# A bidirectional ConvLSTM scan in 128-row products, with shifted taps loaded ahead and the cell in column halves

## What is computed

```python
def step(carry, xr):                       # xr: one row, (16, 48, 32)
    h, c = carry
    inp = jnp.concatenate([xr, h], axis=1)
    gates = lax.conv_general_dilated(inp, w_mid, (1,), 'SAME', dimension_numbers=dn) + b[None, :, None]
    i, f, g, o = jnp.split(gates, 4, axis=1)
    c2 = jax.nn.sigmoid(f) * c + jax.nn.sigmoid(i) * jnp.tanh(g)
    h2 = jax.nn.sigmoid(o) * jnp.tanh(c2)
    return ((h2, c2), h2)
```

## Time and profile before

| | us |
|---|---|
| median of 3 runs (636.04 to 639.83) | 638.73 |
| profiled execution | 642.67 |
| its span, first to last instruction | 640.9 |
| TensorE busy in the span (90%) | 574.0 |
| VectorE (78%), ScalarE (68%), POOL (39%) | 500.4, 435.9, 251.7 |
| chain that ended last, share: TensorE, VectorE, issue, DMA | 47%, 28%, 10%, 6% |

### The profile page before, as it was taken

The page is one execution under the profiler, slowest core; times in us unless marked ns, Lnnn a source line. Parts: engine busy times, 40 slices in busy tenths (PEclk is TensorE's granted clock), DMA queues, the critical chain, the costliest instruction groups (busy, mean ns, idle before and its releaser), DMA issues.

```text
span 640.9 us, 12616 instructions
## 1 busy us (share of the span) xinstructions
PE 574.0 (90%) x3404; PEld 340.9 (53%) x3404; DVE 500.4 (78%) x962; ACT 435.9 (68%) x645; POOL 251.7 (39%) x299
## 2 busy tenths in 40 slices
PE   6993699999999999979979989999999999999970
PEld 1232366666665556555545656666666556555530
DVE  2687669999999979997998657666667677776765
ACT  3771369999999969877886655555555556565645
POOL 2660004333333323333866634444444434343410
PEclk9996689999999979998997999999999999999985
DMA  8857646655656776777531233333322222222316
GB/s 216 260 148 220 185 118 141 140 141 141 141 142 156 153 146 155 145 137 152 132 76 32 48 82 86 80 79 79 78 64 68 76 77 80 78 67 65 96 55 197
DMA packets 101751, 75.77 MB, mean 118 GB/s; under 512 B 52883, under 2 KB 85141, under 8 KB 101381
## 3 DMA queue, kind: packets, MB, share of 16 engines
q1 hardware_dynamic: 100948, 71.69, 45.3%
q10 hardware_dynamic: 768, 3.67, 2.3%
HBM read 48.84 MB, written 22.15 MB: 111 GB/s over the span
## 4 chain that ended last, share of the span: by engine, by line
PE 47%; DVE 28%; issue 10%; DMA 6%; SPq 3%; ACT 2%; DVEq 1%; POOL 1%; ACTq 0%; POOLq 0%
DVE hmax L1242 11%; PE pz L724 10%; PE pz L703 9%; PE pz L718 5%; DVE onehot L1227 5%; PE p_edge L724 5%; PE p_edge L703 4%; DVE idx L1218 3%; PE p_edge L718 3%; PE pz L554 3%; PE pz L632 2%; DMA idx_d<-idx 2%; DMA y_hl<-y_d 2%; DVE val L1210 2%; PE p_keys L546 1%
## 5 line engine op out<-in xcount | busy, mean ns | idle before, releaser
L1242 DVE TENSOR_REDUCE hmax<-gel 96x128 f32<-96x1024 f32 x128 | 151.7, 1203 | 16.6 <-ACT gel L849 16.6
L849 ACT ACTIVATE gel<-pz 96x1024 f32<-96x1024 f32 x128 | 130.5, 1020 | 37.8 <-PE pz L632 27.6
L1119 POOL CAST ht<-h 48x512 fp32r<-48x512 f32 x62 | 37.5, 605 | 141.9 <-DVE h L1353 141.3
L1121 POOL TENSOR_TENSOR ht<-h,ht 48x512 fp32r<-48x512 f32 x62 | 73.5, 1185 | 5.0
L724 PE MATMUL pz<-ht,w_xh 128*112 128x512 f32 x258 | 71.9, 414 | 1.6 <-DMA ht<-xh 1.6
L703 PE MATMUL pz<-xh,w_xh 128*112 128x512 f32 (+1 forms) x258 | 69.1, 404 | 0.0
L632 PE MATMUL pz<-onehot,ab_hi 64*96 64x512 f32 x256 | 61.3, 475 | 4.0 <-ACT gel L849 3.4
L914 ACT ACTIVATE pz<-c 48x512 f32<-48x512 f32 x43 | 25.7, 597 | 48.0 <-DVE c L1346 48.0
L724 PEld LDWEIGHTS pz<-ht,w_xh 128*112 128x112 f32 x258 | 41.9, 175 | 28.4 <-issue 14.7
L703 PEld LDWEIGHTS pz<-xh,w_xh 128*112 128x112 f32 x258 | 45.7, 178 | 16.8 <-issue 0.7
L632 PE MATMUL pz<-onehot,ab_lo 64*96 64x512 f32 x256 | 53.4, 412 | 0.0
(11 more groups left out here) (148 smaller groups left out, 1219.3 us busy)
## 6 DMA issues: line engine op xcount, KB each, us to landing
ib<-idx_d SPq DMA_DIRECT2D x64, 256.0 KB, 4.3
y_d<-y SPq DMA_DIRECT2D x32, 192.0 KB, 3.3
y_hl<-y_d SPq DMA_DIRECT2D x32, 192.0 KB, 4.1
hist_d<-h SPq DMA_DIRECT2D x62, 96.0 KB, 1.9
hp<-hist_d SPq DMA_DIRECT2D x30, 192.0 KB, 2.7
kr<-xn_d SPq DMA_DIRECT2D x32, 98.0 KB
xn_d<-x_in SPq DMA_DIRECT2D x32, 96.0 KB, 2.3
kl<-xn_d SPq DMA_DIRECT2D x32, 96.0 KB
```

The source lines that it names most:

```text
L849: act.activation(gel[:, t % 2], pz[0:O, 2 * (t % 2):2 * (t % 2) + 2, :], ACT.Gelu) \
L1119: pool.tensor_copy(h_slots(ht, 0, d), columns(h2[0:C, d])).then_inc(S["h_top"], 1)
L1121: pool.tensor_tensor(h_slots(ht, HALF, d), columns(h2[0:C, d]), h_slots(ht, 0, d).bitcast(F32), ALU.subtract).then_inc(S["h_lo"], 1)
L1242: dve.tensor_reduce(dst, gel[:, t % 2].rearrange("p w (r c k) -> p w r c k", r=WS, k=KN), AX_X, ALU.max).then_inc(S["maxed"], 1)
```

## The change

The products with 48 rows, `w_e` and `he` are gone. `x_part` becomes two products of 98 rows (three shifted copies of 32 rows of the low part of x and two rows of ones for the bias, in the new tile `xt`). `h_part` has six products on `xh` and six on `ht`, all with 128 rows; the head of h now goes into the low rows of `xh` of the next row, its rest and its rounded copy into `ht`. Before that the low parts of x are stored to DRAM (`store_lows`, `xl_d`); `load_shifts` loads the three shifted copies two steps ahead, `load_thirds` two pieces for `ht` one step ahead. The stores of the lows and the twins of three quarters of the rows move into SP's turns for groups 14 to 21 and 26 to 29, the last quarter into steps 2 to 5. In the turns, y is loaded for g + 4 before the spread. Cell, its tanh (now into `cu`), h and its head are computed in two column halves. All loops of the scan are unrolled. The bias, scaling and splitting of the weights follow the new rows.

```diff
@@ SP @@
+            def store_lows(r, sem):
+                for first, rows, src in ((0, C, 0), (C, HALF - C, HALF + 32)):
+                    sp.dma_start(xl_d[r:r + 2, first:first + rows].rearrange("r c n -> c r n"),
+                                 xh[src:src + rows, r:r + 2, 0:SLOT - 1].bitcast(F32)).then_inc(S[sem], 16)
...
+            def load_shifts(s, d):
+                lows = xl_d[row_of(s, d), 0:32, 0:SLOT - TAPS]
+                sp.dma_start(xt[0:96, d, s % 2, 0:SLOT - TAPS].bitcast(F32),
+                             bass.AP(lows.tensor, lows.offset, [[1, TAPS], [SLOT - 1, 32], [1, SLOT - TAPS]])) \
+                    .then_inc(S[f"x_shifts{d}{s % 2}"], 16)
+            def load_thirds(s, d):
+                for q in range(2):
+                    sp.dma_start(ht[HALF * q + C:HALF * q + HALF, d, 0:SLOT - 1].bitcast(F32),
+                                 xl_d[row_of(s, d), 32 + 16 * q:C + 16 * q]).then_inc(S[f"x_third{d}"], 16)
...
-                for k, stage in ((3, load_y), (0, load_xres), (3, store_idx), (-2, store_x1), (5, load_keys),
+                for k, stage in ((0, load_xres), (3, store_idx), (-2, store_x1), (5, load_keys), (4, load_y),
                                  (3, spread_idx)):
...
+                    if at < 8:
+                        block, part = divmod(at, 4)
+                        sp.wait_ge(S["x1_split"], PAIRS * (block + 1))
+                        store_lows((0, 24)[block] + 2 * part, "xl_stored0")
+                        load_twins((0, 24)[block] + 2 * part, "x_twins0")
+                    if 12 <= at < 16:
+                        sp.wait_ge(S["x1_split"], PAIRS * 3)
+                        store_lows(16 + 2 * (at - 12), "xl_stored1")
+                        load_twins(16 + 2 * (at - 12), "x_twins1")
...
-            def step(s, b):
+            def step(s):
                 for d in range(2):
-                    if not isinstance(s, int) or s + 1 < H:
-                        load_third(s + 1, d)
-                    if isinstance(s, int) and s + 2 < H // 2:
-                        load_twins(s + 2, d, b)
+                    if s + 1 < H:
+                        sp.wait_ge(S["gates"], s * 4 + (2 * d + 2))
+                        load_thirds(s + 1, d)
+                    if s + 2 < H:
+                        load_shifts(s + 2, d)
                     store_h(s, d)
-                    if isinstance(s, int) and 2 <= s < H // 2 + 2:
-                        load_x1r(s - 2, d)
-                if later(s, H // 2 + 1):
-                    load_h(s - 1, 1 - b)
+                    if 6 <= s < H // 2 + 6:
+                        load_x1r(s - 6, d)
+                    if 2 <= s < 6:
+                        (store_lows, load_twins)[d](4 + 2 * s, ("xl_stored1", "x_twins1")[d])
+                if s >= H // 2 + 1:
+                    load_h(s - 1, 1 - s % 2)
@@ TensorE @@
+            def x_part(s, d, k):
+                pe.wait_ge(S[f"x_shifts{d}{s % 2}"], s // 2 * 16 + 16)
+                for m in range(2):
+                    pe.matmul(gate_banks(k, d)[m][0:TOP, :], w_x[0:98, d, m], by_column(xt[0:98, d, s % 2, 0:(W + 1) * B]),
+                              start=True, stop=False)
+            def h_part(s, d, k):
+                if later(s):
+                    pe.wait_ge(S["h_top"], s * 4 + (2 * d - 2))
                 for m in range(2):
                     for t in range(TAPS):
+                        row = xh[:, reg(row_of(s, d), 0, 1), t:t + (W + 1) * B].rearrange("p o n -> p (o n)")
+                        pe.matmul(gate_banks(k, d)[m][0:TOP, :], w_rows[:, 0, d, m, t], by_column(row),
+                                  start=False, stop=False)
+                pe.wait_ge(S[f"x_third{d}"], s * 32 + 32)
                 if later(s):
                     pe.wait_ge(S["h_edge"], s * 2 + (d - 1))
                     pe.wait_ge(S["h_lo"], s * 2 + (d - 1))
                 for m in range(2):
                     for t in range(TAPS):
+                        mm = pe.matmul(gate_banks(k, d)[m][0:TOP, :], w_rows[:, 1, d, m, t],
+                                       by_column(ht[:, d, t:t + (W + 1) * B]), start=False, stop=(t == TAPS - 1))
                     mm.then_inc(S["gates"], 1)
@@ ScalarE @@
             def tanh_cell(s, d, k):
-                act.wait_ge(S["cells"], s * 2 + (d + 1))
-                act.activation(gate_banks(k, d)[1][HALF:TOP, :], c2[HALF:TOP, d], ACT.Tanh, scale=0.5) \
-                    .then_inc(S["tanh_c"], 1)
+                for n, (to, c) in enumerate(zip(column_halves(cu[HALF:TOP, d]), column_halves(c2[HALF:TOP, d]))):
+                    act.wait_ge(S["cells"], s * 4 + (2 * d + 1 + n))
+                    act.activation(to, c, ACT.Tanh, scale=0.5).then_inc(S["tanh_c"], 1)
@@ POOL, h_parts @@
+                for n, h in enumerate(column_halves(h2[0:C, d])):
+                    pool.wait_ge(S["h2_ready"], s * 4 + (2 * d + 1 + n))
+                    pool.tensor_copy(head[:, BX * n:BX * n + BX], columns(h)).then_inc(S["h_top"], 1)
+                pool.wait_ge(S["h_top"], s * 4 + (2 * d + 2))
+                pool.tensor_tensor(h_slots(ht, 0, d), columns(h2[0:C, d]), head.bitcast(F32),
                                    ALU.subtract).then_inc(S["h_lo"], 1)
@@ VectorE, cell @@
+                for to, kept, new in zip(column_halves(c2[HALF:TOP, d]), column_halves(cu[HALF:TOP, d]),
+                                         column_halves(b_if[HALF:TOP, :])):
+                    dve.scalar_tensor_tensor(to, kept, 0.5, new, ALU.mult, ALU.add).then_inc(S["cells"], 1)
...
+                for n, (to, out_gate, cell_tanh) in enumerate(zip(column_halves(h2[0:C, d]),
+                                                                  column_halves(tgo[HALF:TOP, d]),
+                                                                  column_halves(cu[HALF:TOP, d]))):
+                    dve.wait_ge(S["tanh_c"], s * 4 + (2 * d + 1 + n))
+                    dve.scalar_tensor_tensor(to, out_gate, 1.0, cell_tanh, ALU.add, ALU.mult) \
+                        .then_inc(S["h2_ready"], 1)
```

More of the change, by code:

```diff
@@ L428, in turn @@
                     sp.wait_ge(S["x1_hi"], 2 * PAIRS)
[L429 to L432, removed]
-                for k, stage in ((3, load_y), (0, load_xres), (3, store_idx), (-2, store_x1), (5, load_keys),
+                    sp.wait_ge(S["pads_set"], 8)
+                    sp.wait_ge(S["xl_stored0"], 32 * 8)
+                    load_shifts(0, d)
+                    load_thirds(0, d)
+                    load_shifts(1, d)
+                for k, stage in ((0, load_xres), (3, store_idx), (-2, store_x1), (5, load_keys), (4, load_y),
                                  (3, spread_idx)):
@@ L519, in _ @@
-            for s in range(14, 18):
-                step(s, s % 2)
-            with sp.Fori(0, H // 4 - 2) as j:
-                for b in range(2):
-                    step(j * 2 + (18 + b), b)
+            consts = ((wp_sb[:], wp), (wp_low[:], wp[C:O]), (gb_sb[:], gb), (comb_sb[:], comb))
+            for s in range(6, 30):
+                step(s)
+                if s < 10:
+                    dst, src = consts[s - 6]
+                    sp.dma_start(dst, src).then_inc(S["consts2"], 16)
@@ L526, in _ @@
                     .then_inc(S["first_loaded"], 16)
-            step(30, 0)
+            step(30)
             load_h(30, 0)
@@ L707, in h_part @@
                 if later(s):
-                    pe.wait_ge(S["h_top"], s * 2 + (d - 1))
                     pe.wait_ge(S["h_edge"], s * 2 + (d - 1))
-                def moving(t, rows, k):
-                    return t[rows, d, k:k + (W + 1) * B].rearrange("p (b w) -> p b w", w=W + 1)[:, :, 0:W]
-                if later(s):
-                    for t in range(TAPS):
-                        for m, src in ((0, ht), (1, he)):
-                            rows = slice(HALF * m, HALF * m + C)
-                            pe.matmul(gate_banks(k, d)[m][0:TOP, :], w_e[rows, d, m, t], moving(src, rows, t),
-                                      start=False, stop=False)
@@ L771, in _ @@
                     pe.wait_ge(S["wp_ready"], 1)
-                step(s, s, twins_of(s), twins_of(s + 1))
+                step(s, s)
             project(14, 0, 7)
@@ L1143, in _ @@
             pool.wait_ge(S["x1_split"], GROUPS)
-            with pool.Fori(1, H // 2 - 1) as j:
-                for b in range(2):
-                    for d in range(2):
-                        h_parts(j * 2 + b, d)
-            for d in range(2):
-                h_parts(30, d)
+            for s in range(2, H - 1):
+                if s == 7:
+                    pool.wait_ge(S["xl_stored1"], 32 * 8)
+                for d in range(2):
+                    h_parts(s, d)
         @block.vector
```

199 lines of the change are left out of this document (95 added, 104 removed).

## The result

The changed kernel takes 646.0 us (median of 4 runs, 641.7 to 650.6) against 638.7 before: ratio 1.013, 95% interval 1.008 to 1.018. 614 was forecast, with a range of 599 to 631. The profiled execution took 645.12 us, with a span of 643.1. An execution more than 1.5% above the fastest of its kernel is left out; there was one, of 687.9 us, in the fourth experiment.

A forecast was written before the change was run, and what follows sets the result against it. TensorE's products were taken to bound the scan, with the chain setting steps without projection after the change; -28.3 in the scan and +3.8 in the turns gave -24.5, so 638.7 became 614 us, range 599 to 631.

The forecast's parts named there:

- SP in the scan: SP's DMA issues: five per half-step, 2.1 to 3.2 of 3.6 us; thirds land in 2.0 and hide.
- rival (e): Scan: late thirds set the pace, slower than now from landings of 4.6; 9.4 a step at 5.5, 669 us; chance 0.07.
- the four terms: Forecast by stretch: start to step 1 +4.3, steps 1 to 17 -14.4, steps 17 to 31 -14.1, the end -0.3 us.
- Products: TensorE in the scan: 14 products of 0.238 us, 3.33 per half-step and 6.67 per step if nothing else waits.
- rival (d): TensorE: 98 rows count as another shape, two changes per half-step cost up to 0.2 each; 627 us; chance 0.08.
- Chain: Scan steps without projection: the chain of one direction through h sets 7.2 us, between 6.8 and 7.6.
- Rival (b): VectorE waits for POOL's subtraction when h is due, up to 0.75 more a step; +22, 636 us; chance 0.07.
- rival (c): Better on both counts: halves at 0.38, no collision, SP hides its extra work; 600 us; chance 0.16.
- Steps with projection: Scan steps 17 to 31: 7.9 us each, between 7.8 and 8.2; -14.1 over the stretch.
- 1.5 us once, after step 1: Scan: SP stands at the wait for the last x1 group with the thirds queued behind it; 1.5 us, an estimate.
- Turns: Turns before the scan: SP's extra work +12, waits for y gone -8.2; sum +3.8 us, between -8.2 and +16.
- Rival (a): Turns before the scan: SP paces them harder, landings stay at 5.5, nothing hides; +16, 626 us; chance 0.12.

The follow-up runs named there:

- the fourth experiment: Changed kernel with every shift loaded twice: once cut over all engines, once unread and listed as 3 taps of 32 rows; 680.0 us, ratio 1.068.
- the first run: Changed kernel with the shift transfer listed as 32 rows of 3 taps, so cut over all engines; 614.7 us, ratio 0.961.
- fifth experiment: Changed kernel with the loads of `hp` issued half a step sooner, shifts still cut in three; 633.4 us, ratio 0.990.
- the ninth experiment: Kernel of the first run with `hp` loaded half a step sooner and SP's last x1 wait behind the thirds of step 3; 613.5 us, ratio 0.966.
- seventh experiment: Kernel before with only the column halves of cell, its tanh, h and POOL's head; 637.0 us, ratio 1.000.

## Why the prediction was wrong

**The step that failed** is "SP in the scan". It counted SP's issues and took 2.0 us for a third from the earlier trace rows, "so they hide with over a us to spare". The one word for the shifts themselves stands under rival (e): "the added traffic is spread evenly". It was spread over three of sixteen engines. 2.0 was measured where no such shift was queued; in the changed kernel a third lands after 2.9 (median) and the store of h after 5.2 instead of 1.9. The list in the diff, with 3 in front, was there to be read. And `hp` has no term at all: in the earlier trace rows a projection is priced by its products, not by when its data come. In the kernel before the first load was issued at 495.09 and first used at 499.63 (timeline, and tile `hp` from 495.0 to 495.8 us):

```profile
495.09 0.79 SPq L471 DMA_DIRECT2D hp<-hist_d  x2
...
499.63 1.08 PE L735 MATMUL p_keys<-hp,wp_sb 96*64 96x512 f32 x4
...
DMA to landing us min/median/max: 2.5/2.7/2.9
```

The second half, issued at 495.45, was there at about 498.3, so 1.3 us were to spare. In the changed kernel the first pair lands after up to 6.1. That margin was never set beside anything that the change puts in the queue. What the runs showed in place of the step: with the shift cut over all engines the same transfers land in 2.0 to 2.6, and the time falls by 31 us.

**Rival (e) had the right kind of failure at the wrong place.** It has late transfers setting the pace, slower than before, from landings of 4.6 on. The thirds did make TensorE wait, most in steps 2 to 7 where the stores of the lows pass too (10.2 of the weight loads' 18.8 us, 363 to 412 us). But 20.0 of the 30.3 us that part the changed kernel's span from the first run's came in steps 17 to 31, 12.6 of them won back by an earlier `hp` (fifth experiment), and its price (669) assumed every step to be hit.

**The other terms came out near their size,** as the first run shows. That its 614.7 stands beside 614 is partly luck. By the spans it gains 28.1, not 24.5; the four terms missed by -3.2, -1.3, +1.4 and -0.6; and the forecast took its starts from an execution 3.9 above the median.

- *Products.* 14 x 0.238 per half-step, without a gap at the 98-row ones. In the timeline of that run the runs of six `ht` products, two x products and six `xh` products last 1.42, 0.49 and 1.43 from start to start:

```profile
441.23 1.59 PE L750 MATMUL p_edge<-ht,w_rows 128*112 128x512 f32 x6
...
442.65 0.65 PE L732 MATMUL pz<-xt,w_x 98*112 98x512 f32 x2
...
443.14 1.59 PE L742 MATMUL pz<-xh,w_rows 128*112 128x512 f32 x6
...
444.57 1.58 PE L750 MATMUL pz<-ht,w_rows 128*112 128x512 f32 x6
```

  So rival (d) is out.
- *Chain.* 7.2 was forecast, 6.98 came. Two halves take 0.76 together, not 2 x 0.44: each takes 0.42, and the second starts 0.34 after the first. And POOL's head did not wait for the second h half, as the prediction had it; it runs beside it (same run):

```profile
441.56 0.76 DVE L1397 SCALAR_TENSOR_TENSOR h<-tgo,cu 48x256 f32<-48x256 f32 x2
...
442.05 0.88 POOL L1160 CAST xh<-h 48x256 fp32r<-48x256 f32 x2 [1.11 <-DVE h L1397]
```

  Over that run the first half of the head takes 0.53 and the second 0.39 (medians), so beside VectorE it is 0.14 longer; the earlier trace rows, a long operation with two SBUF operands, was the wrong row for a short one. Rival (b) needs POOL's subtraction to run when h is due. Here it ends at 444.20 and the next h starts at 445.28, so its condition doesn't arise; step 2, below, is the exception. The halves came as rival (c) had them, 0.38 each.
- *Steps with projection.* 7.9 forecast, 8.00 measured.
- *1.5 us once, after step 1.* Step 2 takes 8.64 against 6.98. The size was about right and the cause wrong: the ninth experiment moved SP's wait and step 2 stayed as it was. In its timeline the last x1 group's operations on POOL stand ahead of the head, which starts at 367.82, though the first half of h is there at 366.32; and the second half of h waits beside one of them (in the section below). No run moved these operations, so this cause is read and not tried. The kernel before has a long step 2 too: 9.74 against 8.1.
- *Turns.* +3.8 was forecast with bounds of -8.2 and +16. The `ht` products of step 1 start 2.7 later than before in the changed kernel and 1.1 later in the first run. In the eight kernels with the change's turns that start lies between 351.1 and 360.9, and with the turns of before it is 353.0 in one and 348.1 in the other (seventh experiment), so single profiles can't judge this term closer. Rival (a) didn't come: the last index store is issued at 320.8, against 319.4 before. The waits for y are gone, as said; but a wait for the keys came in their place (after, 81 to 345 us), which the prediction didn't have and whose cause no run tried:

```profile
PE p_keys L609 <- DMA kr<-xn_d: 11.3, 7, 2.5
```

## What to carry to other kernels

For every new transfer read, beside its bytes and its issue time, how long the first dimension of its list is on either side: here a list that begins with 3 ran on three of sixteen DMA engines. Then list what is queued behind it and how much time each of these has between landing and use; in this kernel the old transfers paid, not the new one. And the shorter chain was worth nothing here until the products were fewer, so price parts of a change together where one uncovers the other.

## What the runs showed of the hardware

- A transfer on three engines delays well-cut transfers on the same queue: the store of h went from 1.9 to 5.2 us, and to 6.8 where a well-cut shift passed beside each badly cut one.
- Two operations of 256 columns in a row on VectorE take 0.76 together, little more than the 0.69 of one with 512: each takes 0.42, but the second starts 0.34 after the first.
- POOL in front of VectorE. The prediction said that no row shows it; the ninth experiment has one, in step 2:

```profile
365.90 1.31 DVE L1398 SCALAR_TENSOR_TENSOR h<-tgo,cu 48x256 f32<-48x256 f32 x2
...
365.96 0.96 POOL L1113 TENSOR_TENSOR xh<-x1t,x1c 48x256 fp32r<-48x256 f32 x1
```

  The first half of h starts at 365.90 and takes 0.42. POOL's subtraction with two SBUF operands starts at 365.96, ahead of the second half at 366.25. That second half takes 0.96 (same run; ns min/median/max of the two halves):

```profile
L1398 DVE SCALAR_TENSOR_TENSOR h<-tgo,cu x2: 422/692/962, 365.9 to 366.2; 48x256 f32<-48x256 f32 x2
```

  It ends 0.28 after the subtraction, which itself takes 0.96 instead of the 0.74 of the earlier trace rows. The first run's step 2 shows the same lengths. That VectorE stood still until POOL had ended fits these times; they don't show it beyond that.
